# A quantized gated network with per-tile weights: the order of the first tiles is changed

## The chip, the cores and the metric

The kernel runs on one core of a Trainium2 chip. The metric is the device time of one execution in microseconds. Of the kernel before, three runs took 830.33 to 831.53 us, median 831.01 us.

TensorE (PE) multiplies; VectorE (DVE), ScalarE (ACT) and GpSimd (POOL) work elementwise; SyncE (SP) and GpSimd issue DMAs. Each engine works through its own list in order, and they wait for each other on semaphores.

## The reference

```python
# B = 32 tiles of 128 x 2048, K = 8 experts
h = gelu(gelu(cond @ W0 + b0) @ W1 + b1)
att = softmax(h @ W2 + b2)                                   # (32, 8)
y = einsum('boi,bih->boh', einsum('bk,koi->boi', att, weight), x) + att @ bias_k
y = bf16(y)
qg, sg = quant(y * inv_gate)          # per row: s = max|.| / 127, q = round(. / s)
qu, su = quant(y * inv_up)
gate = (qg @ w_gate.T) * sg * s_wgate                        # 2048 -> 1024
up   = (qu @ w_up.T) * su * s_wup
inter = bf16(clip(silu(gate) * up, -10, 10))
qi, si = quant(inter * inv_inter)
out = x + (qi @ w_down.T) * si * s_wdown                     # 1024 -> 2048
```

## The kernel before

Each of the 32 tiles t goes through the same stages. Its weight matrix (128 x 128) is the sum of the eight experts, each times its attention (`aggregate`). TensorE multiplies it with the tile's x (`conv`, four banks of 512 columns); ScalarE evacuates (`conv_out`) to y. VectorE multiplies y by the two rows of factors and finds each row's scale (`quant_g`, `quant_u`); ScalarE makes the codes (`quant_g`, `quant_u` there). The codes are turned so that the contraction lies on the partitions: for tiles 0 to 3 by TensorE (`turn_g`, `turn_u`, `turn_i`) with an evacuation by ScalarE (`turned_g` and so on), from tile 4 on by a transposing DMA of SP and a fix by ScalarE (`fix_g`, `fix_u`, `fix_i`). `gate` and `up` are 32 matmuls of 512 columns each, `down` four banks of 8. VectorE scales gate and up out of PSUM (`gate_out`, `up_out`), ScalarE applies Silu, VectorE multiplies, clips, and finds the third scale (`inner_head`, `inner_tail`); at the end `result(t, c)` scales a bank of `down` and adds it to x in place (`down_out` L1166, `residual` L1171). SP stores the tile and loads a later x into the same slot; there are four slots.

From tile 4 on a fixed round is kept: gate t, half of up t, `down(t-1, 0)`, the other half, the other banks of `down(t-1)` with conv t+2 between them. The first tiles have an order written out by hand in each engine's list, since the weights are still arriving. GpSimd loads `wg`, `wu` and `wd` in four parts each, casting them; each part of `wd` waits until the first tiles have left its place, since their y, codes and products live in it (`Y_HOME`, `QGT_HOME`, `QUT_HOME`, `XU_HOME`). Tile 1's product with the gate factors lives in the slot of x 3 (`XG_HOME`), so SP issues x 3 (L337) once its codes are made. GpSimd also spreads five rows of factors over the partitions, out of a place in `wd`.

The sums of the experts go four ways: tile 0 by five VectorE steps, the rest by ScalarE diagonals (L765) and matmuls (L481); tile 1 by eight ScalarE diagonals, matmuls and a copy (L771); tiles 2 and 3 by a VectorE operation that makes the diagonals (L997), matmuls and a copy; the others by GpSimd (L406 to L414). Six matmuls on filler data (L652) run ahead of the first real ones.

The lines around the change: waits for conv L488 to L512, for gate L544 to L565, for down L626 to L645; TensorE's order L650 to L721; ScalarE's from L849; VectorE's from L1173.

## Time and profile before

| | |
|---|---|
| median of three runs | 831.01 us |
| the profiled execution: time | 831.8 us |
| its span | 830.0 us |
| PE busy | 802.8 us (97%) |
| DVE, ACT, POOL busy | 715.8, 441.4, 143.5 us |
| mean granted clock of TensorE | 0.992 |
| L564 gate and up, 128 x 512 matmuls | 206.8 and 202.4 us |
| L644 down, 128 x 512 matmuls | 211.2 us |
| L1171 residual, mean | 707 ns |

The page's chain that ended last puts 88% of the span on PE. PE's busy time counts matmuls whose ends are modelled, and a matmul at half clock counts as busy too; so the stretches in which PE is not busy and those with a lower clock have to be looked for in the timeline. A share of busy time over the whole span says little here, as the first 155 us differ from the rest.

### The profile page before, as it was taken

To read this page: it belongs to the slowest core of one execution; us is meant where nothing else is said; L and a number is where in the kernel's file an instruction comes from. 1 tells how busy PE (TensorE), PEld (TensorE's weight loads), DVE (VectorE), ACT (ScalarE), POOL (GpSimd) and SP (SyncE) were. 2 spreads that over 40 slices of the span, in tenths; PEclk is the share of its full clock that TensorE was granted. 3 is DMA by queue.
4 is the path that set the end of the run, shared out by engine and by line. 5 is a ranking of instruction groups with operands and counts; after the bars stand their busy time and mean duration, and the time that the engine had idled before them with its cause. 6 is when DMAs were issued, how large, how long until landed. Compare 5 with 4: busy or idle time off the path is not lost.

```text
span 830.0 us, 9248 instructions
## 1 busy us (share of the span) xinstructions
PE 802.8 (97%) x3556; PEld 368.9 (44%) x3556; DVE 715.8 (86%) x810; ACT 441.4 (53%) x385; POOL 143.5 (17%) x136
## 2 busy tenths in 40 slices
PE   7789896999999999999999999999999999999997
PEld 4434442444444444444444444444444444444443
DVE  6955789699888889988888998888899888888968
ACT  5666223555566555456654545655454566545441
POOL 1600050222012222201222220122222102222000
PEclk9989998999999999999999999999999999999999
DMA  9972724465444545445355444435545444554332
GB/s 297 241 155 51 152 101 151 140 148 158 118 142 121 166 148 156 140 121 146 115 165 159 145 141 126 146 108 165 164 141 140 138 140 107 162 164 140 94 111 101
DMA packets 158340, 118.76 MB, mean 143 GB/s; under 512 B 147540, under 2 KB 147668, under 8 KB 148823
## 3 DMA queue, kind: packets, MB, share of 16 engines
q1 hardware_dynamic: 156568, 105.59, 42.3%
q0 software_dynamic: 1728, 12.58, 7.4%
q8 instruction: 28, 0.46, 0.2%
q14 instruction: 16, 0.13, 0.1%
HBM read 60.48 MB, written 33.55 MB: 113 GB/s over the span
## 4 chain that ended last, share of the span: by engine, by line
PE 88%; DMA 5%; DVE 4%; ACT 2%; issue 1%; DVEq 0%; ACTq 0%
PE gate_ps L564 26%; PE up_ps L564 25%; PE down_ps L644 23%; PE conv_ps L510 12%; DMA xt<-x 2%; DMA wd<-w_downT 1%; DVE xt L1171 1%; DMA out<-xt 1%; PE gate_ps L644 1%; DVE down_sc L1166 1%; ACT qg L751 0%; DVE xt L1020 0%; PE conv_ps L515 0%; ACT wd L796 0%; DVE part_max L1081 0%
## 5 line engine op out<-in xcount | busy, mean ns | idle before, releaser
L644 PE MATMUL down_ps<-wd,qiT 128*128 128x512 bf16 x896 | 211.2, 379 | 0.0
L564 PE MATMUL gate_ps<-wg,qgT 128*128 128x512 bf16 x928 | 206.8, 380 | 0.0
L564 PE MATMUL up_ps<-wu,quT 128*128 128x512 bf16 x896 | 202.4, 379 | 0.0
L1002 DVE TENSOR_REDUCE amax<-region 128x1 f32<-128x2048 f32 (+1 forms) x90 | 173.0, 1923 | 1.2
L406 POOL TENSOR_TENSOR prod<-wexp,att_bc 128x1024 f32<-128x1024 f32 x28 | 53.4, 1907 | 538.4 <-DVE region L1060 527.7
L644 PEld LDWEIGHTS down_ps<-wd,qiT 128*128 128x128 bf16 x896 | 87.6, 98 | 123.3 <-issue 29.7
L564 PEld LDWEIGHTS gate_ps<-wg,qgT 128*128 128x128 bf16 x928 | 91.0, 98 | 111.3 <-issue 3.8
L564 PEld LDWEIGHTS up_ps<-wu,quT 128*128 128x128 bf16 x896 | 87.7, 98 | 105.7
L510 PE MATMUL conv_ps<-xt,aggw 128*128 128x512 f32 x244 | 118.6, 610 | 11.4 <-DMA xt<-x 10.4
L751 ACT ACTIVATE qg<-region,recip 128x2048 f16<-128x2048 f32 x30 | 60.0, 2002 | 122.0 <-DVE recip L1012 117.7
L740 ACT ACTIVATE y<-conv_ps,aggb 128x512 bf16<-128x512 f32 x118 | 80.9, 687 | 75.2 <-PE conv_ps L510 70.3
L1171 DVE TENSOR_TENSOR xt<-xt,down_sc 128x512 f32<-128x512 f32 x128 | 90.5, 707 | 3.5
L1166 DVE SCALAR_TENSOR_TENSOR down_sc<-down_ps,scale,swd_bc 128x512 f32<-128x512 f32 x118 | 87.6, 742 | 1.5 <-PE down_ps L644 1.5
L1113 DVE SCALAR_TENSOR_TENSOR region<-up_ps,scale,swu_bc 128x1024 f32<-128x1024 f32 x28 | 35.9, 1284 | 49.3 <-PE up_ps L564 49.3
L846 ACT ACTIVATE qiT<-qiT 128x1024 bf16<-128x1024 f16 x28 | 29.6, 1057 | 84.2 <-DMA qiT<-qi 84.2
L510 PEld LDWEIGHTS conv_ps<-xt,aggw 128*128 128x128 f32 x244 | 46.8, 194 | 53.0 <-issue 31.1
L781 ACT ACTIVATE qu<-region,recip 128x2048 f16<-128x2048 f32 x30 | 60.1, 2003 | 19.1 <-DVE recip L1012 19.1
L1057 DVE TENSOR_TENSOR region<-y,invg_bc 128x2048 f32<-128x2048 bf16 x27 | 61.7, 2285 | 8.0 <-ACT qi L828 8.0
L1060 DVE TENSOR_TENSOR region<-y,invu_bc 128x2048 f32<-128x2048 bf16 x27 | 61.7, 2285 | 0.0
L810 ACT ACTIVATE qgT<-qgT 128x2048 bf16<-128x2048 f16 x28 | 53.5, 1910 | 9.8 <-DMA qgT<-qg 9.7
L814 ACT ACTIVATE quT<-quT 128x2048 bf16<-128x2048 f16 x28 | 53.3, 1903 | 4.8 <-DMA quT<-qu 4.8
L1099 DVE SCALAR_TENSOR_TENSOR region<-gate_ps,scale,swg_bc 128x1024 f32<-128x1024 f32 x29 | 37.2, 1284 | 2.8 <-PE gate_ps L564 2.5
(162 smaller groups left out, 570.2 us busy)
## 6 DMA issues: line engine op xcount, KB each, us to landing
xt<-x SPq DMA_DIRECT2D x31, 1024.0 KB, 4.8
out<-xt SPq DMA_DIRECT2D x30, 1024.0 KB, 4.0
wg<-w_gateT POOLq DMA_DIRECT2D x4, 1024.0 KB, 19.4
wu<-w_upT POOLq DMA_DIRECT2D x4, 1024.0 KB, 16.8
wd<-w_downT POOLq DMA_DIRECT2D x4, 1024.0 KB, 8.8
invg_bc<-inv_gate SPq DMA_DIRECT2D x1, 1024.0 KB, 8.0
out<-xt SPq DMA_DIRECT2D x2, 512.0 KB, 2.7
xt<-x SPq DMA_DIRECT2D x2, 512.0 KB, 3.9
```

Source lines behind the costliest of these rows:

```text
L510: nc.tensor.matmul(conv_bank(t, c), aggw[t % 2][:, :], xcols(t, c), start=True, stop=True).then_inc(conv_done, 1)
L564: last = nc.tensor.matmul(acc[:, n * BANK:(n + 1) * BANK], codes[:, k * P:(k + 1) * P], wts[:, k, n * BANK:(n + 1) * BANK], start=(k == 0) ...
L644: last = nc.tensor.matmul(down_bank(t, c), qiT_at(t)[:, k * P:(k + 1) * P], wd[:, k, c * BANK:(c + 1) * BANK], start=(k == 0), stop=(k == ...
L740: nc.scalar.activation(y_at(t)[:, c * BANK:(c + 1) * BANK], conv_bank(t, c), ACT.Identity, bias=aggb[:, t:t + 1]).then_inc(y_ready, 1)
L751: nc.scalar.activation(qg[:, :], xg_at(t), ACT.Copy, scale=trecip(t, 0), bias=ROUND).then_inc(gcodes_ready, 1)
L781: nc.scalar.activation(qu[:, :], xu_at(t), ACT.Copy, scale=trecip(t, 1), bias=ROUND).then_inc(ucodes_ready, 1)
L810: nc.scalar.activation(qgT[:, :], qgT16, ACT.Copy, bias=-ROUND).then_inc(qgT_ready, 1)
L1002: nc.vector.tensor_reduce(amax[:, i:i + 1], src, axis=AX.X, op=ALU.max, apply_absolute_value=True).then_inc(max_ready, 1)
L1057: nc.vector.tensor_tensor(region1[:, :], y[:, :], invg_bc[:, :], ALU.mult).then_inc(xg_ready, 1)
L1060: nc.vector.tensor_tensor(region2[:, :], y[:, :], invu_bc[:, :], ALU.mult).then_inc(xu_ready, 1)
L1166: nc.vector.scalar_tensor_tensor(down_sc[c % 2], down_bank(t, c), tscale(t, 2), swd_bc[:, c * BANK:(c + 1) * BANK], ALU.mult, ALU.mult).th ...
L1171: nc.vector.tensor_tensor(xcols(t, c), xcols(t, c), down_sc[c % 2], ALU.add).then_inc(result_ready, 1)
```

## The change

It moves work of the first six tiles and some memory. Tile 1's gate product goes into a part of `wd`, and x 3 waits for the first part of `wg` only. The rows to spread go into `wu`, whose loads wait for the spreads. Tile 0's sum takes six VectorE steps and two diagonals, tile 1's eight VectorE steps ahead of `quant_first`, and tile 2's diagonals move behind it. Fillers are four. Tile 1's up codes move to another part of `wd`, the loads of `wd` get another order, and `down(0, c)` reads its parts in that order. Down 2 gets banks of its own. Conv 5 stands behind all of gate 4. ScalarE's and VectorE's orders follow.

```diff
-        XG_HOME = [region1[:, :], xt[:, (XS - 1) * H:XS * H]]
+        XG_HOME = [region1[:, :], wd[:, :, :].rearrange("p k h -> p (k h)")[:, 6 * H:8 * H].bitcast(fp32)]
-        QUT_HOME = [wd_part(3, bf16), wd_part(4, bf16), quT[:, :], qgT[:, :]]
+        QUT_HOME = [wd_part(3, bf16), wd_part(2, bf16), quT[:, :], qgT[:, :]]
-        rows_s = wd[:, :, :].rearrange("p k h -> p (k h)")[:, 4 * H:8 * H].bitcast(fp32)[0:1, :]
+        rows_s = wu[:, KH // 2:KH, :].rearrange("p k i -> p (k i)").bitcast(fp32)[0:1, :]
-        SPLIT = 5
+        SPLIT = 6
...
                       [bank(gate_ps, 0), bank(gate_ps, 1), bank(down_ps, 0), bank(down_ps, 1)],
+                      [bank(up_ps, 0), bank(up_ps, 1), bank(down_ps, 0), bank(down_ps, 1)]]
...
-            sp.wait_ge(gcodes_ready, 2)
+            sp.wait_ge(wg_in[0], 16)
             sp.dma_start(xslot(3), x[3, :, :]).then_inc(x_in[3], 16)
...
+            pool.wait_ge(row_spread, SWD)
             for i in range(WCH - 1):
                 load(wu, w_upT, i, wu_in)
...
             load(wd, w_downT, 0, wd_in)
-            pool.wait_ge(up_done, 1)
-            load(wd, w_downT, 1, wd_in)
+            pool.wait_ge(gate_done, 3)
+            load(wd, w_downT, 2, wd_in)
             pool.wait_ge(ucodes_ready, EARLY + 1)
             load(wd, w_downT, 3, wd_in)
             pool.wait_ge(up_done, 2)
-            load(wd, w_downT, 2, wd_in)
+            load(wd, w_downT, 1, wd_in)
...
                     if t == 0:
                         pe.wait_ge(agg_step, SPLIT + 1)
+                    elif t == 1:
+                        pe.wait_ge(agg_step, SPLIT + 1 + K)
...
                     elif t == EARLY + 1:
-                        pe.wait_ge(scaled_ready, NC * 2 + 2)
+                        pe.wait_ge(scaled_ready, NC + 2)
...
+                        if t == EARLY + 1:
+                            pe.wait_ge(scaled_ready, NC * 2 + 2)
...
                 elif t == 2:
-                    pe.wait_ge(scaled_ready, NC + c + 1)
+                    if c == 0:
+                        pe.wait_ge(upval_ready, EARLY + 1)
+                    elif c >= 2:
+                        pe.wait_ge(scaled_ready, NC + c + 1)
...
+                ks = (0, 1, 4, 5, 6, 7, 2, 3) if t == 0 else range(KI)
...
-            for _ in range(6):
+            for _ in range(4):
...
-            aggregate_mm(1)
             conv(1)
...
+            turn_g(2)
             turn_u(0)
             gate(0, range(12, KH))
             gate(1, range(12, KH))
-            turn_g(2)
             gate(2)
+            turn_g(3)
             turn_u(1)
-            turn_g(3)
             gate(3)
...
-            conv(5, range(2))
             for t in range(4, B):
                 gate(t, HALVES[0])
+                gate(t, HALVES[1])
                 if t == 4:
-                    conv(5, range(2, NC))
-                gate(t, HALVES[1])
+                    conv(5)
...
             diagonals(0)
-            diagonals(1)
             conv_out(0)
-            aggregate_out(1)
...
             conv_out(3)
-            turned_u(0)
             quant_g(2)
             turned_g(2)
+            turned_u(0)
             quant_u(1)
             silu(0)
             quant_g(3)
-            silu(1)
-            turned_u(1)
             turned_g(3)
             quant_u(2)
+            turned_u(1)
+            silu(1)
             silu(2)
...
             quant_u(4)
-            conv_out(5, range(2))
             fix_u(4)
-            conv_out(5, range(2, NC))
+            conv_out(5)
             quant_i(3)
...
+            def aggregate_second():
+                w = aggw[1][:, :]
+                for k in range(K):
+                    if k == 0:
+                        op = nc.vector.tensor_scalar(w, wexp[:, 0, :], att_col(1, 0), None, ALU.mult)
+                    else:
+                        dve.wait_ge(agg_step, SPLIT + 1 + k)
+                        op = nc.vector.scalar_tensor_tensor(w, wexp[:, k, :], att_col(1, k), w, ALU.mult, ALU.add)
+                    op.then_inc(agg_step, 1)
...
             aggregate_first()
             biases(0, FIRST)
-            diagonals(2)
+            aggregate_second()
...
             quant_first()
+            diagonals(2)
             diagonals(3)
...
-            result(2, 0)
-            result(2, 1)
             quant_u(4)
-            result(2, 2)
+            for c in range(NC - 1):
+                result(2, c)
             inner_tail(3)
```

## Rows read from the trace of the kernel before

**Rows 1.** Busy time by stretches: PE, PEld, DVE, ACT, POOL, clock, DMA share, GB/s.

```profile
100.00:150.00 50.00, 41.08 (x175) 17.97 (x174) 40.97 (x46) 15.61 (x14) 10.87 (x8) 0.93 0.36 114
...
200.00:300.00 100.00, 100.00 (x433) 45.22 (x432) 90.40 (x99) 54.60 (x45) 18.11 (x17) 1.00 0.47 144
```

**Rows 2.** Waits from 150 us on: us in total, times, longest.

```profile
DVE region L1113 <- PE up_ps L564: 48.4, 25, 2.0
```

**Rows 3.** Timeline of the start: start us, duration us, engine, line, operation, [idle before].

```profile
7.97 1.51 DVE L985 SCALAR_TENSOR_TENSOR aggw<-wexp,att_bc,aggw 128x128 f32<-128x128 f32 x4
...
9.20 1.49 PE L481 MATMUL gate_ps<-wexp,region 128*128 128x128 f32 x6
...
18.93 0.16 DVE L1012 RECIPROCAL recip<-scale 128x1 f32<-128x1 f32 x1
...
26.85 1.94 PE L510 MATMUL conv_ps<-xt,aggw 128*128 128x512 f32 x4
```

**Rows 4.** Timeline: x 3's issue, gate 1's first half, conv 3.

```profile
30.33 0.35 SPq L337 DMA_DIRECT2D xt<-x  x1
...
33.86 3.63 PE L564 MATMUL up_ps<-wg,wd 128*128 128x512 bf16 x16 [0.71 <-ACT wd L740]
...
41.32 5.40 PE L510 MATMUL conv_ps<-xt,aggw 128*128 128x512 f32 x8 [3.83 <-DMA xt<-x]
```

**Rows 5.** Lines L396 and L335: wg's issues; landings of its first, its last two, x 2.

```profile
L396 POOL DMA_DIRECT2D wg<-w_gateT x4: 550/556/859, 8.5 to 10.4; - x4
...
DMA to landing us min/median/max: 12.1/12.1/12.1
...
DMA to landing us min/median/max: 21.6/24.4/27.2
...
DMA to landing us min/median/max: 19.7/19.7/19.7
```

**Rows 6.** Timeline: xg_product(3), gate 2, gate 3.

```profile
54.58 2.29 DVE L1020 TENSOR_TENSOR region<-y,invg_bc 128x2048 f32<-128x2048 bf16 x1 [9.11 <-ACT qg L751]
...
58.13 8.77 PE L564 MATMUL gate_ps<-wg,wd 128*128 128x512 bf16 x32 [2.52 <-DVE down_sc L1099]
...
70.38 7.07 PE L564 MATMUL up_ps<-wg,qgT 128*128 128x512 bf16 x32 [1.70 <-ACT qgT L788]
```

**Rows 7.** Timeline: the last load of wd and down(0, 0).

```profile
93.34 0.53 POOL L396 DMA_DIRECT2D wd<-w_downT  x1 [6.75 <-PE up_ps L564]
...
103.61 2.76 PE L644 MATMUL down_ps<-wd,qg 128*128 128x512 bf16 x12 [2.35 <-DMA wd<-w_downT]
```

**Rows 8.** Timeline: the last residual of tile 0.

```profile
110.96 1.61 DVE L1171 TENSOR_TENSOR xt<-xt,down_sc 128x512 f32<-128x512 f32 x1
```

**Rows 9.** Timeline of tile 4's entry: codes, store 1, conv 5, gate 4, down(3, 0).

```profile
128.68 2.00 ACT L751 ACTIVATE qg<-region,recip 128x2048 f16<-128x2048 f32 x1 [4.22 <-PE down_ps L644]
...
132.57 0.47 SPq L358 DMA_DIRECT2D out<-xt  x1
...
134.56 1.91 ACT L810 ACTIVATE qgT<-qgT 128x2048 bf16<-128x2048 f16 x1 [3.88 <-DMA qgT<-qg]
...
141.86 3.78 PE L510 MATMUL conv_ps<-xt,aggw 128*128 128x512 f32 x4 [6.37 <-DMA xt<-x]
...
145.43 4.69 PE L564 MATMUL gate_ps<-wg,qgT 128*128 128x512 bf16 x16
...
152.46 1.14 ACT L828 ACTIVATE qi<-region,recip 128x1024 f16<-128x1024 f32 x1
...
156.37 1.06 ACT L846 ACTIVATE qiT<-qiT 128x1024 bf16<-128x1024 f16 x1 [2.77 <-DMA qiT<-qi]
...
158.58 1.89 PE L644 MATMUL down_ps<-wd,qiT 128*128 128x512 bf16 x8
```

**Rows 10.** Timeline of the steady part: a transposing DMA's issue and the fix behind it.

```profile
165.44 1.32 SPq L349 DMA_TRANSPOSE quT<-qu  x1
...
170.93 1.91 ACT L814 ACTIVATE quT<-quT 128x2048 bf16<-128x2048 f16 x1 [1.04 <-DMA quT<-qu]
```

More of the change, by code:

```diff
@@ L478, in aggregate_mm @@
                 for k in ks:
-                    if t < 2:
-                        pe.wait_ge(diag_act, k - SPLIT + 1 if t == 0 else K - SPLIT + k + 1)
+                    if t == 0:
+                        pe.wait_ge(diag_act, k - SPLIT + 1)
                     last = nc.tensor.matmul(agg_ps[t], diag_part(t, k), wexp[:, k, :], start=(k == ks[0]), stop=(k == K - 1))
@@ L635, in down @@
                 elif t == 2:
-                    pe.wait_ge(scaled_ready, NC + c + 1)
+                    if c == 0:
+                        pe.wait_ge(upval_ready, EARLY + 1)
+                    elif c >= 2:
+                        pe.wait_ge(scaled_ready, NC + c + 1)
                 else:
                     pe.wait_ge(scaled_ready, NC * t + c - 1)
-                for k in range(KI):
+                ks = (0, 1, 4, 5, 6, 7, 2, 3) if t == 0 else range(KI)
+                for k in ks:
                     if t == 0 and c == 0 and k % (KI // WCH) == 0:
@@ L644, in down @@
                     last = nc.tensor.matmul(down_bank(t, c), qiT_at(t)[:, k * P:(k + 1) * P],
-                                            wd[:, k, c * BANK:(c + 1) * BANK], start=(k == 0), stop=(k == KI - 1))
+                                            wd[:, k, c * BANK:(c + 1) * BANK], start=(k == ks[0]), stop=(k == ks[-1]))
                 last.then_inc(down_done, 1)
@@ L760, in diagonals @@
             def diagonals(t):
-                if t == 0:
-                    act.wait_ge(ident_set, 2)
-                    act.wait_ge(att_dve, ATT[0])
-                for k in range(SPLIT if t == 0 else 0, K):
+                act.wait_ge(ident_set, 2)
+                act.wait_ge(att_dve, ATT[0])
+                for k in range(SPLIT, K):
                     nc.scalar.activation(diag_part(t, k), ident[:, :], ACT.Copy, scale=att_col(t, k)).then_inc(diag_act, 1)
             def aggregate_out(t):
-                act.wait_ge(agg_mm, t + 1 if t < 2 else POOLED)
-                if t >= 2:
-                    act.wait_ge(conv_done, NC * (t - 1))
+                act.wait_ge(agg_mm, POOLED - 1)
+                act.wait_ge(conv_done, NC * (t - 1))
                 nc.scalar.activation(aggw[t % 2][:, :], agg_ps[t], ACT.Copy).then_inc(agg_out, 1)
@@ L993, in diagonals @@
                     dve.wait_ge(ident_set, 2)
-                else:
-                    dve.wait_ge(agg_mm, 2)
                 a = att_bc[:, t * K:(t + 1) * K].unsqueeze(2).to_broadcast([P, K, P])
@@ L1029, in xu_product @@
                     dve.wait_ge(row_spread, INVU)
[L1030 removed]
+                    dve.wait_ge(agg_mm, 2)
                 elif t == 2:
[L1032 removed]
+                    dve.wait_ge(gcodes_ready, 2)
                 elif t == EARLY + 1:
```

17 lines of the change are left out of this document (7 added, 10 removed).

## The prediction

> **What bounds the kernel now.** I read the busy time by stretches first [rows 1]. In the steady part TensorE is busy 100 of 100 us at clock 1.00; between 100 and 150 us it is busy 41.08 of 50 at 0.93. VectorE has room in the steady part: it waited for `up_ps` 25 times, 48.4 us in all, about 1.9 us a tile [rows 2]. So from tile 4 on the end of the kernel is TensorE's, and a microsecond gained before the first matmul of `down(3, 0)` (158.58 us [rows 9]) is gained at the end, if the others keep up. Then I read TensorE's timeline of the start, for each idle stretch and what ended it. There are five large ones: 3.83 us for x 3 [rows 4], 2.52 us for `gate_out(0)` and 1.70 us for a turned tile [rows 6], 2.35 us for the last part of `wd` [rows 7], 6.4 us for x 5 [rows 9]. After three of them TensorE ran at half clock: conv 3 took 5.40 us instead of 3.8 (1.94 a half [rows 3]), gate 2 took 8.77 instead of 7.07, conv 5's first half 3.78 instead of 1.9 and gate 4's first half 4.69 instead of 3.6 [rows 4, 6, 9]. Idle and slow stretches make about 23 us. The change aims at all of them.
>
> I lay the new order out against the trace, engine by engine, with the durations of the rows, and note when each step comes now.
>
> **Start (about -0.7 us, a loss).** `aggregate_first` gets a sixth step of 0.38 us (1.51 us for four [rows 3]) and TensorE two matmuls less than the six that took 1.49 us; with two fillers less it is through at 9.6. So conv 0 starts at about 10.3 instead of 11.2. Tile 1's sum, which was 8 ScalarE diagonals, 16 matmuls and a copy, becomes 8 VectorE steps, 8 x 0.38 = 3.0 us, and they stand before `quant_first`: 10.65 to 13.65. That pushes `quant_first` by 0.5 us, although its first chunk is ready: its reciprocal comes at 19.6 instead of 19.1 [rows 3]. `diagonals(2)` (1.2 us) now also stands between it and `quant_g(1)`, whose reciprocal goes from 28.3 (2.0 us of codes ahead of x 3's issue at 30.33 [rows 4]) to about 29.5. TensorE is ahead (conv 1 ends at 17.8) but in order, waits 3 us for tile 0's codes at 20.8, does its diagonals' matmuls, and conv 2 starts at 27.5 instead of 26.85 [rows 3].
>
> **x 3 early (gain 4.2 us at the end of conv 3).** The slot of x 3 no longer holds tile 1's product, so SP issues it when the first part of `wg` has landed, at 8.5 + 12.1 = 20.6 [rows 5], not at 30.33 [rows 4]. SP has nothing else queued. Before, it took 10.9 us beside the weight loads. x 2 lands at 24.7 (5.0 + 19.7 [rows 5]); if x 3 moves only behind it, it is there at 24.7 + 10.9 = 35.6. The last two parts of `wg` landed at 31.5 and 37.6 [rows 5]; x 3 can push the third to 37, and it is first read at 42.5. Gate 1's first half starts at 35.1 (33.86 before [rows 4]: the 1.25 us of the start), so conv 3 starts at 38.7, x 3 waiting, and at full clock it ends at 42.5 instead of 46.7. The `wu` loads now wait for all row spreads, by 0.2 us, and are needed at 68: nothing.
>
> **ScalarE's order (gain 6.1 us more at gate 3).** Before, `xg_product(3)` waited 9.11 us for `quant_g(2)` [rows 6], which stood behind conv 3's evacuation and `turned_u(0)`. Now `quant_g(2)` comes first: 43.2 to 45.2. VectorE comes from `quant_u(1)` at 46.8, so `xg_product(3)` is over at 49.1, gate 0 at 49.6, `gate_out(0)` at 51.1; TensorE gets to gate 2 at 51.3. The wait of 2.52 us and the half clock behind it go. Gate 2 ends at 58.3; ScalarE has loaded Silu's table, done `silu(0)` and `quant_g(3)` by 56.6, the turns for gate 3 are done at 60.1, and gate 3 runs from 60.1 instead of 70.38 [rows 6]. `silu(1)` and `turned_u(1)` are moved behind; up 1 is due at 75, they are done at 66. If ScalarE's chain slipped by 1 us, gate 3 would too.
>
> **wd's parts (gain 2.4 us).** Up 0 starts at 68.0, up 2 ends at 90.1. Part 1 of `wd` is now the last load: it waits for `up(1)`, at 83.0, and its k 2 and 3 are read last in `down(0, 0)`, at 90.05 + 6 x 0.22 = 91.3. The last load took 10.2 us before because two others were in flight (93.34 to 103.57 [rows 7]); alone, as now, the nearest is that stretch less the time in which it waited for the others, some 7.5 us: 90.5. No wait. By 10.2 us it would be 93.2, and 1.9 us of the gain would be lost.
>
> **x 4 takes some back (-1.5 us).** `up(3)` ends at 104.5, 12.6 us earlier. But x 4's slot is free only after tile 0's results. VectorE starts `up_out(2)` at 90.2, and results 0 end about 101.5, as GpSimd's two sums run beside them as before (112.57 before [rows 8]: its last residual took 1.61 us, the mean of all is 0.71). Stores and reloads add 4.5 us: conv 4 starts at 106.0 and is over 11.0 us earlier than before, as is all behind it up to the end of down 2, 124.4 instead of 135.5. Down 2's new banks take away gate 4's wait for tile 2's results; its first two wait for `up_out(3)` at 106.4, its others for tile 1's last results at 119.4 and 120.8, and it needs them at 121 and 122.5.
>
> **Conv 5 behind gate 4 (gain 7.0, then -2.4 us).** Gate 4 waits for `qgT` alone. That took 7.8 us from the end of down 1 (128.6, the quantization, the transpose's 3.88 us, the fix until 136.47 [rows 9]), so 117.6 + 7.8 = 125.4: 1.0 us of idle, and then gate 4 in 7.0 us at full clock. x 5 came 9.3 us behind tile 1's store (132.57 to 141.86 [rows 9]); now 121.5 + 9.3 = 130.8, and conv 5 starts at 132.4. `quant_u(4)` now goes ahead of results 2: codes at 128.6, its transpose at 132.6 if it takes 3.9, fixed at 134.5. ScalarE evacuates conv 5 only behind that fix, so conv 5's third bank waits 0.9 us and it ends at 137.1, where before up 4 began at about 155.1, 3.45 us ahead of `down(3, 0)`. Queued behind conv 5's evacuation on ScalarE is `quant_i(3)`: last bank out at 137.8, codes 1.14, transpose 2.77, fix 1.06 us [rows 9]: 142.9. TensorE has only half of up 4, 3.5 us, to do meanwhile: it stands at 140.6 and waits 2.3 us. Before, conv 5's end had 7.1 us of work behind it. This new wait has no row. Its bounds: 0 (the transposes land at once) and, since a transpose beside other transfers landed 5.5 us after its issue in the steady part (165.4 to 170.9 [rows 10]), 3.9. I put it and the transpose at 2.5 together, nearer to the 3.88 us row, as x 5 is almost in: `down(3, 0)` starts at 143.1.
>
> **Sum.** 158.58 - 143.1 = 15.5 us: +4.2 +6.1 +2.4 -1.5 +7.0 -2.5 is 15.7, less rounding. The profiled execution has a span of 830.0 us and a time of 831.8; the median shown is 831.01. 831.0 - 15.5 = **815.5 us**. After that point ScalarE and VectorE are 1 us nearer to TensorE than before (`quant(5)` starts 14.7 us earlier, TensorE 15.5); the least slack that I find behind it is 0.45 us at `down(3, 3)`, and each tile gives VectorE 1.9 us back.
>
> **Rivals.**
> The likeliest, as above, 60%: 815.5, with its own range of 813.5 to 817.
>
> The clock, 22%. TensorE has new idle stretches, 3.0 us before tile 0's turn and 2.4 before `down(3, 0)`. In the trace an idle stretch of 2.52 us was followed by half clock and 1.7 us were lost; one of 2.35 us was not [rows 6, 7]. For: both are of that size. Against: with fewer fillers conv 0 may run slower, which fills the first. One costs 1.7, both 3.4: 817.2 to 818.9.
>
> Shorter chains, 9%. If x 4 and the new wait cost half, 1.5 / 2 + 2.5 / 2 = 2 us, and gate 4's idle 1 us goes: 812.5. For: ScalarE's pieces are short. Against: each is in order.
>
> x 2 is late, 5%. If x 3's packets were served beside x 2's, x 2 could land 5 us later, at 30, against 27.5 for conv 2, and all behind it with it: 818 to 820. For it speaks that x 2 already took 19.7 us from its issue [rows 5]. The Trainium skill ("DMA: Bandwidth & Descriptors", Queues, rings and completion order) says that a DMA engine takes one ring's descriptors in order, and that queues alternate by packet; by that rule x 2 keeps its time and only `wg` pays. No row shows two transfers of x issued this far apart beside the loads, so the chance stays small.
>
> Slower, 2%: VectorE and ScalarE, now 1 us nearer, end last in every steady tile. Tiles 4 to 30 are 27 tiles of about 24 us; from 0.6 us a tile on, 27 x 0.6 = 16.2 us, the gain is gone: 832 or more. Against: VectorE's 90.40 of 100 us [rows 1].
>
> No difference, 2%: the gain is given back before tile 6 by a wait that I don't see, 830 to 832.
>
> **How the numbers follow.** Forecast 815.5. The low end takes in most of the shorter chains, the high end both clock losses and half of the late x 2: 812 to 820, about 8.5 in 10. A difference of 0.2% (1.7 us) is what a measurement of this kernel can tell. Faster 0.96, same 0.02, slower 0.02.
>
> **What would show it.** Right: conv 3 without a DMA wait and at full clock near 39; gate 2 near 51; gate 3 near 60; `down(0, 0)` in one piece; conv 4 held 1 to 2 us by x 4; conv 5 without a wait for x; a wait of `down(3, 0)` for ScalarE's fix, 2 to 4 us; 100% busy behind it. Wrong: idle TensorE in the steady tiles, half clock after 20 us, or a wait for `wg`, or `down(0, 0)` still waiting for `wd`.

## The result and the profile after

Of the changed kernel, four runs took 820.36 to 822.53 us, median **821.84 us**; four of the kernel before, on the same chip, 830.33 to 831.53, median 830.76. The ratio is 0.9889 (0.9872 to 0.9906). The forecast was 815.5 us with a range of 812 to 820. The direction was right, but the time lies outside the range: the kernel gained 8.9 us of the 15.5. The profiled execution took 821.92 us, with a span of 820.1; the span gained 9.9 us.

First the page of the kernel after: its span and its busy times.

```profile
span 820.1 us, 9140 instructions
...
PE 794.7 (97%) x3469; PEld 366.1 (45%) x3536; DVE 721.3 (88%) x819; ACT 437.5 (53%) x375; POOL 142.3 (17%) x136
```

The same stretches as in [rows 1], with 0 to 100 us ahead of them (us, then the busy time of PE, PEld, DVE, ACT and POOL, TensorE's clock, DMA share, GB/s).

```profile
0.00:50.00 50.00, 40.84 (x190) 22.26 (x193) 43.30 (x66) 28.14 (x38) 16.13 (x20) 0.97 0.97 258
50.00:100.00 50.00, 49.65 (x290) 25.15 (x293) 37.20 (x37) 26.67 (x24) 5.83 (x7) 1.00 0.59 114
100.00:150.00 50.00, 41.54 (x170) 17.97 (x172) 39.29 (x43) 17.94 (x17) 7.66 (x7) 0.97 0.41 131
200.00:300.00 100.00, 99.58 (x425) 45.23 (x432) 89.30 (x99) 57.54 (x47) 17.40 (x16) 1.00 0.52 141
```

Between 50 and 100 us TensorE now hardly stands still. Between 100 and 150 us it is busy 41.54 us of 50, which is no better than before [rows 1], and there is a loss ahead of 50 us. The steady part is as before. So the missing time must be looked for in two places, with the timeline: the stations of the forecast, in the order of time (start us, duration us, engine, line, operation, [idle before, and what ended it]).

```profile
21.35 2.62 POOL L418 PARTITION_BROADCAST invu_bc<-wu  x1 [9.66 <-issue]
21.72 2.36 DVE L951 TENSOR_TENSOR qi<-qi,qiT 128x224 f32<-128x224 f32 x1
31.25 2.00 ACT L758 ACTIVATE qg<-wd,recip 128x2048 f16<-128x2048 f32 x1 [2.99 <-DVE recip L1022]
33.31 1.07 PE L518 MATMUL down_ps<-ident,qg 128*128 128x128 f16 x16 [2.61 <-ACT qg L758]
41.08 3.87 PE L513 MATMUL conv_ps<-xt,aggw 128*128 128x512 f32 x8
53.47 7.07 PE L567 MATMUL gate_ps<-wg,wd 128*128 128x512 bf16 x32
62.47 6.85 PE L567 MATMUL up_ps<-wg,qgT 128*128 128x512 bf16 x31
...
96.13 1.89 POOL L407 TENSOR_TENSOR prod<-wexp,att_bc 128x1024 f32<-128x1024 f32 x1 [10.38 <-issue]
96.40 2.17 DVE L1181 TENSOR_TENSOR xt<-xt,down_sc 128x512 f32<-128x512 f32 x1
102.61 1.61 DVE L1181 TENSOR_TENSOR xt<-xt,down_sc 128x512 f32<-128x512 f32 x1
108.65 5.40 PE L513 MATMUL conv_ps<-xt,aggw 128*128 128x512 f32 x8 [2.12 <-DMA xt<-x]
...
129.01 1.91 ACT L815 ACTIVATE qgT<-qgT 128x2048 bf16<-128x2048 f16 x1 [5.50 <-DMA qgT<-qg]
130.97 7.08 PE L567 MATMUL gate_ps<-wg,qgT 128*128 128x512 bf16 x32 [2.66 <-ACT qgT L815]
132.84 3.54 SPq L350 DMA_TRANSPOSE quT<-qu  x1
137.89 1.88 PE L513 MATMUL conv_ps<-xt,aggw 128*128 128x512 f32 x4
138.50 1.91 ACT L819 ACTIVATE quT<-quT 128x2048 bf16<-128x2048 f16 x1 [5.69 <-DMA quT<-qu]
148.68 1.90 PE L653 MATMUL down_ps<-wd,qiT 128*128 128x512 bf16 x8 [2.20 <-ACT qiT L851]
```

The five large idle stretches of before are gone: conv 3 does not wait for x 3 [rows 4], gate 2 doesn't wait, and it takes 7.07 us instead of 8.77 [rows 6], gate 3 doesn't wait for a turned tile, `down(0, 0)` does not wait for `wd` [rows 7], and conv 5 does not wait for x 5 [rows 9]. New ones have come: 2.61 us ahead of tile 1's turn, 2.12 ahead of conv 4, 2.66 ahead of gate 4 and 2.20 ahead of `down(3, 0)`. Three steps are dearer than in the forecast. VectorE's step at 21.72 takes 2.36 us for 224 elements per partition, under GpSimd's spread at 21.35. Conv 4 waits 2.12 us and then takes 5.40. Both transposes of tile 4 let ScalarE wait 5.5 to 5.7 us, where [rows 9] has 3.88.

Last, the wait that the "slower" rival named, from 150 us on (us, times, longest):

```profile
DVE region L1123 <- PE up_ps L567: 47.9, 25, 2.3
```

Before it was 48.4 us in 25 times [rows 2]: VectorE still waits for TensorE in the steady tiles. The gain at `down(3, 0)` is 158.58 [rows 9] less 148.68, 9.9 us, and the gain of the span is 830.0 less 820.1, 9.9 us too. In this execution everything is decided before 150 us.

**The ledger.** The starts of six stations on TensorE (us), in the forecast, in the kernel after, and in another execution of the changed kernel (the control of the next section):

| | forecast | after | control |
|---|---|---|---|
| gate 3 | 60.1 | 62.47 | 61.40 |
| `down(0, 0)` | 90.05 | 92.11 | 91.26 |
| conv 4 | 106.0 | 108.65 | 107.90 |
| `down(1, 0)`, behind conv 4 | 110.0 | 113.89 | 111.91 |
| gate 4 | 125.4 | 130.97 | 128.98 |
| `down(3, 0)` | 143.1 | 148.68 | 146.41 |

The 5.6 us that `down(3, 0)` lacks in the kernel after are: 1.2 by `down(0, 0)` in both executions, and 0.85 more in the kernel after (92.11 less 91.26); 0.6 at conv 4's start (2.65 less 2.06); 1.25 in conv 4's own duration (3.9 less 2.65); 1.7 behind that, which the table first shows at gate 4 (5.57 less 3.89). The experiments ask for the cause of each. (Of gate 3's 32 matmuls the kernel after shows 31: the record of the first is missing, and by the steps of the control it started about 0.2 us before 62.47.)

### The profile page after: what moved, and what is told of

It is laid out like the page before. It is cut to its first block, busy times and chain, and to the rows that moved or that the text cites. A ratio compares the mean times of both kernels' runs of the same rounds, so it can differ in the third digit from the quotient of the medians.

```text
span 820.1 us, 9140 instructions
## 1 busy us (share of the span) xinstructions
PE 794.7 (97%) x3469; PEld 366.1 (45%) x3536; DVE 721.3 (88%) x819; ACT 437.5 (53%) x375; POOL 142.3 (17%) x136
## 4 chain that ended last, share of the span: by engine, by line
PE 90%; DVE 5%; DMA 2%; ACT 1%; issue 1%; SPq 0%; DVEq 0%; ACTq 0%
PE gate_ps L567 26%; PE up_ps L567 25%; PE down_ps L653 23%; PE conv_ps L513 13%; PE gate_ps L653 1%; DVE xt L1181 1%; DMA quT<-qu 1%; DMA qgT<-qg 1%; ACT qg L758 0%; PE conv_ps L518 0%; DMA xt<-x 0%; DVE down_sc L1176 0%; PE down_ps L518 0%; DVE wd L1030 0%; DMA qiT<-qi 0%
## 5 line engine op out<-in xcount | busy, mean ns | idle before, releaser
L653 PE MATMUL down_ps<-wd,qiT 128*128 128x512 bf16 x868 | 205.6, 379 | 3.7 <-ACT qiT L851 2.2
L1123 DVE SCALAR_TENSOR_TENSOR region<-up_ps,scale,swu_bc 128x1024 f32<-128x1024 f32 x28 | 35.9, 1283 | 47.9 <-PE up_ps L567 47.9
L851 ACT ACTIVATE qiT<-qiT 128x1024 bf16<-128x1024 f16 x28 | 29.6, 1057 | 81.5 <-DMA qiT<-qi 81.5
L786 ACT ACTIVATE qu<-region,recip 128x2048 f16<-128x2048 f32 x30 | 60.1, 2004 | 15.3 <-DVE recip L1022 15.3
L815 ACT ACTIVATE qgT<-qgT 128x2048 bf16<-128x2048 f16 x28 | 53.5, 1910 | 12.5 <-DMA qgT<-qg 12.5
L833 ACT ACTIVATE qi<-region,recip 128x1024 f16<-128x1024 f32 x30 | 34.2, 1140 | 11.1 <-DVE recip L1022 11.0
## 6 DMA issues: line engine op xcount, KB each, us to landing
wg<-w_gateT POOLq DMA_DIRECT2D x4, 1024.0 KB, 20.1
```

The costliest lines, as they stand in the source:

```text
L653: last = nc.tensor.matmul(down_bank(t, c), qiT_at(t)[:, k * P:(k + 1) * P], wd[:, k, c * BANK:(c + 1) * BANK], start=(k == ks[0]), stop=(k ...
L786: nc.scalar.activation(qu[:, :], xu_at(t), ACT.Copy, scale=trecip(t, 1), bias=ROUND).then_inc(ucodes_ready, 1)
L815: nc.scalar.activation(qgT[:, :], qgT16, ACT.Copy, bias=-ROUND).then_inc(qgT_ready, 1)
```

## The experiments

Each kernel is the changed one with the edit that is shown. Times are medians, and ratios stand against the kernel before on the same chip, with 95% intervals: 833.55 us beside the control, the held spreads, `quant_i(3)` first and `down(1, 0)` ahead; 831.6 beside tile 1's sum on TensorE, the three edits together, the held sums and the held store; 833.67 beside the other four. The four runs of a variant spread over 0.8 to 8.5 us, so several intervals overlap; where they do, the verdict rests on the stations of the profile, one execution each, and not on the time.

### The changed kernel once more

> The changed kernel once more, for how far its stations move from one profiled execution to the next. In the first profile down(3, 0) starts at 148.7 us where 143.1 was forecast. Theory 1 (the miss is systematic: VectorE's softmax step held by a GpSimd spread, 2.36 us instead of 0.39, and x 4's late arrival): the step takes over 2 us again, gate 3 starts at 62 to 63, conv 4 at 108 to 109, down(3, 0) at 147.5 to 149. Theory 2 (the miss is chance, from the clock and transposes): the stations move by over 2 us between the two profiles, and some come near the forecast's 60.1, 106.0 and 143.1. The turned gate codes of tile 4 waited 5.5 us for their transpose, 3.9 before: if that is chance it is near 4 here.

821.13 us, ratio 0.984 (0.9801 to 0.988). Its stations are in the ledger.

```profile
146.41 2.31 PE L653 MATMUL down_ps<-wd,qiT 128*128 128x512 bf16 x8 [2.19 <-ACT qiT L851]
148.51 4.93 PE L567 MATMUL up_ps<-wu,quT 128*128 128x512 bf16 x16
```

The same program differs from itself by 2.3 us at `down(3, 0)`, yet its span is only 0.6 us shorter (819.5 against 820.1). The kernel after had TensorE at half clock from 34.8 to 38 us and from 109.2 to 113 us; the control had neither, though its idle ahead of the first was 2.62 us, the same as 2.61. Instead it was at half clock from 147.8 to 151.2, behind the wait of `down(3, 0)`: `down(3, 0)` and half of up 4 took 6.87 us, where they took 5.19 in the kernel after. So the clock took about 2.1 us in one execution and 1.7 in the other, at different places. Ahead of `down(3, 0)`, 3.3 us of the miss are there without it.

### GpSimd's spreads held until the softmax is over

```diff
+            pool.wait_ge(att_dve, 12)
             (ahead of the first spread)
```

> GpSimd's first spread waits until VectorE has done the second group's three softmax steps (about 1.5 us later than now). Theory 1 (GpSimd's spread holds VectorE's two-input steps): the first step takes 0.4 us instead of 2.36, quant_g(1)'s reciprocal comes at about 29.5 instead of 31.2, TensorE's idle ahead of tile 1's turn shrinks from 2.6 us to 1 to 1.5, and gate 3 starts 1.5 to 2.5 us earlier, at 60 to 61; time 819 to 820.5. Rival (VectorE is held by something else, or the product of tile 1 is then held longer instead): the reciprocal stays at 31 and gate 3 at 62.5; time unchanged, 821 to 822.5.

817.86 us, ratio 0.9803 (0.9773 to 0.9832). The timeline of this kernel:

```profile
21.43 0.39 DVE L952 TENSOR_TENSOR qi<-qi,qiT 128x224 f32<-128x224 f32 x1
...
22.91 4.12 POOL L418 PARTITION_BROADCAST invu_bc<-wu  x1 [10.77 <-DVE qi L956]
...
27.87 1.99 ACT L759 ACTIVATE qg<-wd,recip 128x2048 f16<-128x2048 f32 x1
58.06 2.10 PE L568 MATMUL up_ps<-wg,qgT 128*128 128x512 bf16 x9
```

The step is 0.39 us again, `quant_g(1)` comes 3.4 us earlier than in the kernel after (27.87 against 31.25), and gate 3 starts at 58.06, 3.3 us ahead of the control. VectorE's step was held by the spread; no order was changed, only the spreads and GpSimd's work behind them start later. Now it is the spread that is held: it begins behind VectorE's 128x2048 product, which is under way at 22.59, and takes 4.12 us instead of 2.62. Whoever starts first holds the other up. The Trainium skill ("SBUF — State Buffer", section "SBUF: two separate sides") says this of the port pair that VectorE and GpSimd share: it is locked, not split, by a GpSimd operation or, against a GpSimd operation that reads SBUF, by one of VectorE with two SBUF inputs, and for the whole instruction. The trace agrees: `qi<-qi,qiT` has two inputs in SBUF and lasted until the spread's end (21.72 + 2.36 = 24.08, against 21.35 + 2.62 = 23.97), while the reduction behind it, with one input, took 0.39 us as ever. Gate 3 is even 2 us ahead of the forecast, in part because the durations of before held some of the same cost: VectorE's 128x2048 product behind the softmax took 3.52 us there, 3.24 in the kernel after and 2.29 here.

By `down(3, 0)` this execution is 4.9 us ahead of the control (141.55 against 146.41). The 1.6 us more are luck: its first residual of tile 0 began at 92.22, 0.05 us ahead of GpSimd's sum, and took 0.69 us, so conv 4 waited 0.57 us for x 4 and not 2.22.

### Tile 1's sum on TensorE again

ScalarE's diagonals for tile 1, TensorE's matmuls behind conv 0 and the copy as in the kernel before, with their buffers and waits; all else of the change stays.

```diff
             conv(0)
+            aggregate_mm(1)
             conv(1)
...
             diagonals(0)
+            diagonals(1)
             conv_out(0)
+            aggregate_out(1)
...
-            aggregate_second()
+            diagonals(2)
             quant_first()
-            diagonals(2)
             diagonals(3)
```

> The changed kernel with tile 1's sum as before: ScalarE diagonals, TensorE matmuls, a copy, and tile 2's diagonals ahead of quant_first. Theory 1 (the eight VectorE steps cost by pushing the softmax steps of the second group under GpSimd's first spread): the softmax step begins at 20 to 20.5 and takes 0.4 us, quant_g(1)'s codes begin at 28 to 29 instead of 31.2, gate 3 starts at 59 to 60.5 instead of 61.4 to 62.5; time 1 to 3 us below the changed kernel's, 818 to 820. Rival (the steps on VectorE are a gain for TensorE and ScalarE and the softmax step is late for another reason): gate 3 starts at 61.5 or later, and the time is the same or above, 821 to 823.

817.2 us, ratio 0.9819 (0.9788 to 0.985). The timeline:

```profile
20.51 0.38 DVE L954 TENSOR_TENSOR qi<-qi,qiT 128x224 f32<-128x224 f32 x1
...
21.82 2.30 POOL L418 PARTITION_BROADCAST invu_bc<-wu  x1 [10.76 <-issue]
...
59.53 2.75 PE L565 MATMUL up_ps<-wg,qgT 128*128 128x512 bf16 x12
```

Without VectorE's eight steps the softmax stands ahead of the spread and takes 0.38 us; gate 3 starts 1.9 us ahead of the control. By another way this gives the same answer: `quant_first`'s reciprocal comes at 19.31, against 19.34 in the control, so the eight steps held nothing there by their own 3.0 us; what they cost is that they push another operation under GpSimd's. With the spreads where they are, this part of the change loses time. With the spreads held it need not: gate 3 started at 58.06 there, earlier than here. The rest of this execution's lead (span 813.9 against 819.5) is not this edit's: no half clock behind `down(3, 0)`, and a shorter transpose, to which I come below.

### ScalarE: tile 3's last codes ahead of `fix_u(4)`

```diff
             quant_u(4)
+            quant_i(3)
             fix_u(4)
             conv_out(5)
-            quant_i(3)
             fix_i(3)
```

> ScalarE makes tile 3's inner codes ahead of fix_u(4) and conv 5's evacuation, while it waits for the transpose anyway. Theory (down(3, 0)'s wait is the chain conv 5 out, codes, transpose, fix, as forecast): the wait of 2.2 us at down(3, 0) goes to under 0.3, and everything behind is 2.0 to 2.4 us earlier: about 819.6. Rival (the wait is taken over by another: up 4's codes or VectorE): down(3, 0) starts no more than 0.5 us earlier against conv 5's start, or later tiles wait; time 821 to 822.

820.31 us, ratio 0.9823 (0.9787 to 0.9858); the interval overlaps the control's. At conv 5 this execution was already 1.7 us later than the control, from causes ahead of the edit, so I read from there:

```profile
137.64 1.88 PE L513 MATMUL conv_ps<-xt,aggw 128*128 128x512 f32 x4
...
146.00 1.89 PE L653 MATMUL down_ps<-wd,qiT 128*128 128x512 bf16 x8
```

`down(3, 0)` doesn't wait. From conv 5's start to it are 8.36 us, against 10.79 in the kernel after and 10.51 in the control. The new wait that the forecast named is worth 2.2 to 2.4 us, and its cause is `quant_i(3)`'s place behind conv 5's evacuation.

### `down(1, 0)` ahead of conv 4

```diff
             up(3)
-            conv(4)
             down(1, 0)
+            conv(4)
+            down(1, 1)
             turn_i(2)
-            for c in range(1, NC):
+            for c in range(2, NC):
```

> TensorE does down(1, 0) ahead of conv 4, into its wait for x 4 of 2.1 us. Theory (x 4's arrival is the bound there, as it comes from tile 0's last result on VectorE): conv 4 starts when it did, 108.6, the 1.7 us of down(1, 0) lie ahead of it, TensorE's clock stays full, so the end of down 2 is 1.7 us earlier, or 2.8 us with the half clock after the wait gone: 819 to 820. Rival (conv 4 or the quantization of tile 4 behind it is the bound, VectorE waiting 3.5 us for y): gate 4 starts no earlier, since its codes hang on conv 4 and the end of down 1; gain under 0.7 us.

820.1 us, ratio 0.9835 (0.9788 to 0.9882).

```profile
107.81 1.95 PE L513 MATMUL conv_ps<-xt,aggw 128*128 128x512 f32 x4
...
133.82 1.99 PE L513 MATMUL conv_ps<-xt,aggw 128*128 128x512 f32 x4 [1.10 <-DMA xt<-x]
```

Conv 4 no longer waits, but conv 5 waits 1.10 us for x 5, which didn't move with TensorE. From `down(0, 0)` to `down(3, 0)` are 54.8 us, against 55.15 in the control. Some 0.8 us of that is half clock behind a wait of 2.40 us in the middle of conv 5 (an estimate: `down(3, 0)` came 10.95 us behind the start of `fix_u(4)`, and 10.2 in the kernels without it). The rest of what conv 4's wait had cost came back as the next wait.

### The spreads held, `quant_i(3)` first and `down(1, 0)` ahead, together

> The three edits of the first series together: spreads behind the softmax steps, tile 3's codes ahead of fix_u(4), down(1, 0) ahead of conv 4. If they are independent: 3.3 us (spreads), 2.2 us (codes) and 0.6 to 1.7 us (down 1, less where x 4's wait has shrunk to 0.6 us already), together 6 to 7 us below the changed kernel: 814.5 to 816, gate 3 at 58, down(3, 0) at 139 to 140.5, no wait of ScalarE's fix ahead of it. If one wait stands behind the other (conv 5 then waits for x 5, the store before it unchanged): down(3, 0) at 141 and 817 to 818.

815.99 us, ratio 0.9811 (0.9795 to 0.9827), no better than with the spreads held alone (0.9803).

```profile
136.70 3.38 PE L514 MATMUL conv_ps<-xt,aggw 128*128 128x512 f32 x4 [2.77 <-ACT y L749]
```

Gate 3 started at 59.55 and not at the 58 that was expected: this execution had an idle of 3.02 us ahead of tile 0's turn and ran at half clock behind it, until 23.5. `down(3, 0)` doesn't wait, but conv 5's second half now waits 2.77 us for ScalarE, which stands at the wait for the u codes' transpose, and runs at half clock behind it. From `down(0, 0)` to `down(3, 0)` are 53.96 us, 1.2 less than the control: the three edits don't add, since conv 5's evacuation still stands behind `fix_u(4)`.

### The sums of GpSimd held until tile 0's results are written

```diff
             pool.wait_ge(prod_ready, 2)
+            pool.wait_ge(result_ready, NC)
             aggregate(4)
```

> GpSimd begins tile 4's and tile 5's sums only when tile 0's results are written. Theory (those sums hold VectorE's residuals): each residual takes 0.69 us instead of 0.97 to 2.17, tile 0's results take 5.7 us instead of 8.6, conv 4 waits for x 4 under 0.5 us instead of 2.1 and starts 1.5 to 2.5 us earlier against up 3, with tile 4's sum just in time; time 819 to 820. Rival (the sum of tile 4 is then the late one, or the store and reload of x 4 take longer): conv 4 starts no earlier.

819.4 us, ratio 0.9854 (0.9837 to 0.9872).

```profile
97.31 0.69 DVE L1182 TENSOR_TENSOR xt<-xt,down_sc 128x512 f32<-128x512 f32 x1
...
102.32 2.75 POOL L407 TENSOR_TENSOR prod<-wexp,att_bc 128x1024 f32<-128x1024 f32 x1 [15.66 <-DVE xt L1182]
...
107.85 4.00 PE L514 MATMUL conv_ps<-xt,aggw 128*128 128x512 f32 x8 [0.41 <-issue]
...
136.26 1.91 ACT L820 ACTIVATE quT<-quT 128x2048 bf16<-128x2048 f16 x1 [5.83 <-DMA quT<-qu]
```

All four residuals take 0.69 us instead of 2.17, 0.98, 0.97 and 1.61, tile 0's results 5.6 us instead of 8.6 (95.63 to 104.2), and conv 4 has no wait for x. From up 3's start to conv 4's are 7.48 us, against 9.18 in the kernel after. So most of x 4's lateness is the same hold as the softmax step's, at another place. The kernel after fits it closely: its four residuals ended 0.55, 0.55, 0.53 and 0.55 us behind the end of the GpSimd operation under which each lay (at 98.02, 99.70, 101.38 and 103.67 us), while `down_sc`, which reads PSUM, took 0.74 us under the same sums. GpSimd pays with its first product (2.75 us), which nobody waits for. From conv 4's start on nothing is gained further: 38.6 us to `down(3, 0)`, against 38.5 in the control, although here the transpose of gate 4's codes was short (ScalarE waited 3.85 us for it, 5.48 in the control). The u codes, which took 5.83 us, held the rest.

### Tile 1's store held until gate 4's codes are turned

```diff
             turn_g(EARLY + 1)
+            sp.wait_ge(gturned, 16)
             store(1)
```

> SP issues tile 1's store only when the transpose of tile 4's gate codes has landed. It took 5.4 to 5.5 us in three profiles in which the store was issued 1.9 us behind it, and 3.8 us where the store was issued 3.5 us behind it. Theory (the store's packets share the DMA engines with the transpose): the transpose lands 3.7 to 3.9 us after the codes, gate 4's wait of 2.6 us shrinks to about 1, and x 5 comes about 2 us later, so conv 5 waits for it. Rival (the spread is chance): it stays at 5.4.

821.54 us in a single run.

```profile
126.22 1.91 ACT L816 ACTIVATE qgT<-qgT 128x2048 bf16<-128x2048 f16 x1 [5.43 <-DMA qgT<-qg]
126.22 0.35 SPq L359 DMA_DIRECT2D out<-xt  x1
130.47 5.56 SPq L350 DMA_TRANSPOSE quT<-qu  x1
```

The wait for the transpose is 5.43 us although the store is issued only at its end, at 126.22. The theory that the store's packets slow the transpose falls. The u transpose's issue, behind a store and a reload that are now later, takes 5.56 us, and ScalarE waits 8.13 us for the u codes. Gate 4 ran at half clock for a part here, behind 2.59 us of idle, and took 8.77 us.

### The u transpose issued ahead of x 5's reload

```diff
             store(1)
-            reload(5)
             turn_u(EARLY + 1)
+            reload(5)
```

> SP issues the transpose of tile 4's up codes ahead of the reload of x 5. With the reload just in front of it the issue took 3.1 to 5.6 us on SP (1.32 in the steady part) and the fix waited 5.3 to 8.1 us. Theory (the transpose pays for the transfer in front of it): its issue takes 1.3 us and it lands about 4 us after the codes, fix_u(4) starts 1.5 us earlier, and x 5, issued at about 134, lands 1 to 2 us after the end of gate 4 and holds conv 5: no gain, 821 to 823. Rival (the long issue is of the first transpose of its kind, wherever it stands): issue over 3 us again.

822.35 us in a single run.

```profile
130.87 1.56 SPq L350 DMA_TRANSPOSE quT<-qu  x1
134.57 1.91 ACT L819 ACTIVATE quT<-quT 128x2048 bf16<-128x2048 f16 x1 [3.73 <-DMA quT<-qu]
137.84 3.97 PE L513 MATMUL conv_ps<-xt,aggw 128*128 128x512 f32 x8 [1.76 <-DMA xt<-x]
```

Ahead of the reload, SP's issue of the transpose takes 1.56 us instead of 3.54, and ScalarE waits 3.73 us instead of 5.69: for the u codes the reload is the cause. But conv 5 now waits 1.76 us for x 5, and from gate 4's start to conv 5's are 8.84 us, against 6.92. The queue only decides which of the two is late.

This is the place of the last 1.7 us of the ledger. `down(3, 0)` hangs on the u codes and not on gate 4's: in the kernel after, the control and the kernels with the spreads held, the sum on TensorE, the sums held, the store held and x 3 late, it starts 10.16 to 10.19 us behind the start of `fix_u(4)`. The times from the end of down 2 to `down(3, 0)` follow the second wait and not the first (us):

| | ScalarE's wait for gate 4's codes | for the u codes | end of down 2 to `down(3, 0)` |
|---|---|---|---|
| tile 1's sum on TensorE | 3.78 | 4.10 | 18.25 |
| sums held | 3.85 | 5.83 | 20.32 |
| control | 5.48 | 5.42 | 20.07 |
| kernel after | 5.50 | 5.69 | 20.37 |
| store held | 5.43 | 8.13 | 22.73 |

The forecast had 18.7 for that stretch (124.4 to 143.1).

### Conv 5 placed as before

```diff
+            conv(5, range(2))
                 gate(t, HALVES[0])
+                    conv(5, range(2, NC))
                 gate(t, HALVES[1])
-                    conv(5)
...
+            conv_out(5, range(2))
             fix_u(4)
-            conv_out(5)
+            conv_out(5, range(2, NC))
```

> The changed kernel with conv 5 around gate 4's first half as before, ScalarE's evacuation likewise. Theory (moving conv 5 takes the wait for x 5 away and pays with the wait at down(3, 0)): TensorE waits for x 5 until about 136, 7 to 8 us after down 2, runs at half clock behind it, and down(3, 0) starts without a wait: gate 4's first half 136 to 141, down(3, 0) at 152 to 154 instead of 148.7; 3.5 to 5 us slower than the changed kernel, 825 to 827. Rival (the order is worth little, as other waits take over): under 2 us.

822.8 us, ratio 0.9864 (0.9835 to 0.9893).

```profile
132.88 3.78 PE L513 MATMUL conv_ps<-xt,aggw 128*128 128x512 f32 x4 [6.38 <-DMA xt<-x]
...
148.78 1.89 PE L653 MATMUL down_ps<-wd,qiT 128*128 128x512 bf16 x8
```

The wait of 6.37 us of [rows 9] is back to within a hundredth of a microsecond, with half clock from 130 to 137 us. The start of `down(3, 0)` is 148.78, next to 148.68 in the kernel after, but this execution's transpose of the g codes took 3.79 us and not 5.50. Here, though, `down(3, 0)` hangs on x 5 and neither on those codes nor on the u codes, so I measure from the end of down 2: 22.3 us here, 20.4 in the kernel after, 20.1 in the control and 23.1 before. The move of conv 5 is worth 1.9 to 2.2 us with the u codes as late as they were, and the expectation of 3.5 to 5 was too high. With the u codes in after 4.10 us, as in the kernel with the sum on TensorE (18.25 us), it would be worth 4.0, an estimate.

### x 3 late again

SP issues x 3 when tile 1's gate codes are made, as before.

```diff
-            sp.wait_ge(wg_in[0], 16)
+            sp.wait_ge(gcodes_ready, 2)
```

> The changed kernel with x 3 issued only when tile 1's gate codes are made, as before. Theory (the early x 3 is worth its whole wait): x 3 is issued at about 33.2, takes 10.9 us, lands at 44, so conv 3 starts at 44.1 instead of 40.2 to 41.8, TensorE idles 3 to 4 us and runs at half clock behind it; gate 3 starts 2.5 to 5 us later than in the changed kernel; 824 to 826. Rival (VectorE's chain, late itself, hides x 3: xg_product(3) comes at 48.4 in any case): gate 3 under 1.5 us later, 821 to 823.

827.01 us, ratio 0.9898 (0.9851 to 0.9946).

```profile
44.86 5.55 PE L513 MATMUL conv_ps<-xt,aggw 128*128 128x512 f32 x8 [4.58 <-DMA xt<-x]
...
67.95 6.85 PE L567 MATMUL up_ps<-wg,qgT 128*128 128x512 bf16 x31
```

The wait of [rows 4] is back, larger, with half clock behind it: gate 3 starts 5.5 us later than in the kernel after and 6.3 later than in the control (the record of its first matmul is missing here too). SP issued x 3 at 33.12 us, where it was 30.33 before [rows 4] and is 21.20 in the kernel after: the codes that it waits for are late by the softmax step, so here the early issue is worth more than the 4.2 us of the forecast. The time shows it less well: the ratio is 0.0058 above the control's, 4.8 us, but one of the four runs took 820.32 us, for which there is no trace, and the intervals overlap.

### The parts that proved worth it, together

Tile 1's sum on TensorE, the sums of GpSimd held, `down(1, 0)` ahead of conv 4, and on ScalarE conv 5's first half with `quant_i(3)` ahead of `fix_u(4)`. The held spreads, with the sum on VectorE, are the other cure of the start; I did not run them with these. Of the edit only ScalarE's part is shown, as the others are above:

```diff
             quant_u(4)
+            conv_out(5, range(2))
+            quant_i(3)
             fix_u(4)
-            conv_out(5)
-            quant_i(3)
+            conv_out(5, range(2, NC))
             fix_i(3)
```

> Tile 1's sum on TensorE and ScalarE again, GpSimd's sums held until tile 0's results are written, down(1, 0) ahead of conv 4, and on ScalarE conv 5's first two banks, then tile 3's codes, then fix_u(4), then the last two banks. If the gains found one by one add up: gate 3 at 59.5, conv 4 not waiting for x 4, down(3, 0) at 136 to 139 without a wait for its fix, 811 to 814. If another bound comes up at conv 5 (x 5 late, as down 1 ahead shortens the way to it, or the up codes): down(3, 0) at 140 to 142, 814.5 to 816.

**813.85 us** (813.2 to 814.0), ratio **0.9755** (0.9731 to 0.9779): faster than both kernels. Its stretch from 100 to 150 us:

```profile
100.00:150.00 50.00, 46.41 (x195) 20.21 (x197) 42.43 (x46) 22.70 (x21) 13.99 (x12) 1.00 0.47 150
```

And its timeline:

```profile
105.61 3.93 PE L512 MATMUL conv_ps<-xt,aggw 128*128 128x512 f32 x8
...
123.07 7.08 PE L566 MATMUL gate_ps<-wg,qgT 128*128 128x512 bf16 x32 [0.64 <-ACT qgT L818]
...
135.75 3.63 PE L566 MATMUL up_ps<-wu,quT 128*128 128x512 bf16 x15 [1.90 <-ACT quT L822]
139.21 1.89 PE L652 MATMUL down_ps<-wd,qiT 128*128 128x512 bf16 x8
...
148.70 1.67 PE L652 MATMUL down_ps<-wd,qiT 128*128 128x512 bf16 x7 [0.62 <-DVE down_sc L1184]
```

TensorE is busy 46.41 us of 50 at clock 1.00, against 41.54 at 0.97. From `down(0, 0)` (89.63) to `down(3, 0)` are 49.58 us, against 56.57 and 55.15. The longest wait that is left is 1.90 us for the u codes. Of the 19.4 us gained at `down(3, 0)` against the kernel before the span keeps 17.9: at 148.70 and at 152.38 TensorE waits for VectorE's `down_sc`, 0.89 us together. Of the other kernels only the two with `quant_i(3)` ahead of `fix_u(4)` show it, with 0.5 us each: VectorE is next in line there. The remaining 0.6 us of the 1.5 I did not trace.

## Why the prediction was off

**What bounds the kernel: right.** The gain at `down(3, 0)` came out at the end, 9.9 and 9.9 us; in the control 12.2 of it became 10.5, by the half clock behind that point.

**Start: the step that failed first.** Conv 0 (10.41 against 10.3) and `quant_first`'s reciprocal (19.38 against 19.6) came as forecast. Then I timed `diagonals(2)` and the softmax behind them with the durations of before, and took 29.5 us for tile 1's reciprocal. It came at 31.05. I had moved VectorE's list without laying it against GpSimd's, whose first spread begins at 21.25 in the trace of before already. One step of 0.38 us became 2.36. Held spreads and the sum on TensorE both take this away (gate 3 at 58.06 and 59.53 instead of 61.4). The term was a loss of 0.7 us at conv 2 and 1.25 at gate 1's first half (35.1 for 33.86); in the control that half started at 36.76, 2.9 us later than before. Of the extra, 1.2 us reached `down(0, 0)`, and 2.1 in the kernel after, with the half clock behind the wait. The eight steps were supposed to cost only their own time.

**x 3 early: right.** It was issued at 21.2 (20.6) and landed 12.5 us later, at 33.7 (35.6). Conv 3 waited for no DMA. That x 3's packets would make x 2 late, the rival with 5%, did not come: x 2 landed at 26.0 us instead of 24.7, still ahead of conv 2, which started at 27.04; the forecast had 27.5.

**ScalarE's order: right.** From conv 3's start to gate 2's are 12.4 us (12.6 in the forecast), from gate 2's to gate 3's 8.8 to 9.0 (8.8). The 2.52 us and the half clock behind them are gone.

**wd's parts: right.** `down(0, 0)` ran in one piece at 92.11, 29.6 us behind gate 3; the forecast had 29.95.

**x 4: right in kind, too small.** The forecast took 1.5 us for it. The start of conv 4 was 0.6 us later still, 2.1 in all. I had tile 0's results end 11.3 us behind the start of `up_out(2)`, with GpSimd's sums beside them as before [rows 8]; they ended 11.9 us behind it (92.37 to 104.22), since the first residual now fell under a sum whole (2.17 us). Holding the sums brings conv 4 1.7 us nearer to up 3, so they are the cause of most of it.

**Conv 5 behind gate 4: the second step that failed.** Its move is worth 1.9 to 2.2 us, not 7.0 less 2.5. The new wait of `down(3, 0)` was forecast at 2.3 us and measured 2.20, with the cause named (`quant_i(3)` behind conv 5's evacuation). What failed is the transpose of the u codes: I let it land 3.9 us behind the codes, by the 3.88 us of the gate codes in the one row that I used [rows 9], and it took 5.69. SP issued it 1.6 us behind x 5's reload, and its issue alone lasted 3.54 us. Ahead of the reload ScalarE waited 3.73, as forecast. The prediction named other transfers as a danger and gave 5.5 us [rows 10], but as a bound for the transpose of `qi` alone. The transpose of gate 4's codes was also longer than forecast (5.50 us, gate 4 waited 2.66 instead of 1.0); for `down(3, 0)` that cost about 0.5 us at most, since VectorE's reciprocal of the u codes came at 130.11 and ScalarE began on them at 130.82.

**The rivals.** The clock (22%, 817.2 to 818.9) came in part. In the kernel after the idle ahead of tile 0's turn was 1.44 us and not 3, and `down(3, 0)`'s 2.20 us was harmless; the half clock struck behind two idle stretches that I hadn't named, 2.61 us ahead of tile 1's turn and 2.12 ahead of conv 4, for 2.1 us together. In the control it struck where the rival said, behind `down(3, 0)`'s wait, for the 1.7 us that it said; the other named place, ahead of tile 0's turn, it struck only in the kernels with the three edits together and with the store held. By itself it explains neither: both are 3.3 to 3.5 us late at `down(3, 0)` without it. Shorter chains (9%) fell: x 4 cost 2.1 us and not half of 1.5, and the new wait was not halved. The "slower" rival fell with the wait of 47.9 us. "No difference" fell.

**The range** summed the losses of the clock and half a late x 2. It had no term for a step of VectorE held by GpSimd, and none for a transpose of the u codes behind a reload; the two with the clock are 1.2 + 1.7 + 2.1 = 5.0 of the 5.6 us. Without those two, 2.9 us, the measured 821.84 would be 818.9, an estimate, and inside the range: the clock alone it would have covered.

**What stays open.** When an idle stretch of TensorE brings half clock. Why tile 1's store took 3.8 to 5.8 us until SP could issue the reload behind it, which sets when the reload meets the u transpose. And why the transpose of gate 4's codes takes one of two times. ScalarE's wait for it is 3.76 to 3.88 us in the kernels with the sum on TensorE, with `down(1, 0)` ahead, with the sums held, with all the good parts, with conv 5 as before, with the three edits together, and before; it is 5.35 to 5.50 us in the others, x 3 late and spreads held among them. The store isn't its cause, and it isn't a matter of tile 4 alone: with conv 5 as before, where tile 4's was short, another of the 28 transposes of gate codes took 5.5 us from issue to landing, against a median of 3.7. No edit that I made is in all of one group and in none of the other.

## What to carry to other kernels

When an operation is moved on VectorE, lay its new time against GpSimd's timeline as well as against its own queue: in these traces a VectorE operation with two inputs in SBUF that began under one of GpSimd's spreads or sums lasted until that one ended, or up to its own 0.7 us longer, and a small one on the critical path lost most. The cure was to let GpSimd wait for one of VectorE's counts, where nobody waited for GpSimd. When one wait of a chain is taken away, look for the next transfer or evacuation in line: `down(1, 0)` ahead of conv 4, or the u transpose ahead of x 5's reload, gave next to nothing alone, while the stretch from `down(0, 0)` to `down(3, 0)` shrank by 5.6 to 7.0 us when its waits were taken away together. And of several late steps, find the one on which the next station hangs: gate 4's codes were late for all to see, but `down(3, 0)` hung on the u codes.
